# The attention product normalised in PSUM and split group by group, with two key tiles of the product issued together

## What is computed

```python
q, k, v = heads(x @ Wq, 16), heads(x @ Wk, 4), heads(x @ Wv, 4)      # k and v repeated 4 times
attn = softmax(q @ k.T / sqrt(32));  x = layernorm(x + (attn @ v) @ Wo)
w_scale = max(|weight|, axis=1) / 127;   w_q = clip(round(weight / w_scale), -128, 127)
x_scale = max(|x|, axis=2) / 127;        x_q = clip(round(x / x_scale), -128, 127)
x = layernorm(x + (x_q @ w_q.T) * x_scale * w_scale + bias)
```

## Time and profile before

| | us |
|---|---|
| median of 3 runs | 861.05 (860.06 to 861.08) |
| the profiled execution | 858.5 |
| its span, first to last instruction | 856.7 |
| head, before the first exponential of segment 0 | 41.3 |
| segment 0 | 94.2 |
| segments 1 to 6 | 102.8, 98.8, 98.3, 98.5, 98.3, 102.2 |
| segment 7 | 86.3 |
| tail | 36.0 |

### The profile page before, as it was taken

One profiled execution on the slowest core, in us unless ns is written; L12 is line 12 of the kernel. 1 busy time (PEld: TensorE's weight loads), 2 busy tenths in 40 slices (PEclk: granted clock), 3 DMA queues, 4 the chain that ended last, 5 costly groups with the idle time before them and its releaser, 6 DMA issues.

```text
span 856.7 us, 12297 instructions
## 1 busy us (share of the span) xinstructions
PE 774.4 (90%) x3752; PEld 431.5 (50%) x3752; DVE 698.3 (82%) x1131; ACT 494.5 (58%) x904; POOL 607.6 (71%) x673
## 2 busy tenths in 40 slices
PE   7698999899899998999899998999899998899874
PEld 5444554465456644565445654566445653344441
DVE  4689668789987898888988898878988789779667
ACT  3155566565566656666556556656666645556644
POOL 3365487687785878767876797957877877678935
PEclk9889899999999999999999999999999998889995
DMA  7531123042132223232231322322230421300001
GB/s 217 136 116 38 39 60 96 20 112 63 51 112 50 66 72 98 52 79 83 63 100 41 84 63 60 102 60 78 73 102 27 112 63 50 99 26 26 26 25 49
DMA packets 40897, 61.89 MB, mean 72 GB/s; under 512 B 10385, under 2 KB 12433, under 8 KB 40833
## 3 DMA queue, kind: packets, MB, share of 16 engines
q1 hardware_dynamic: 39488, 57.38, 24.3%
q0 software_dynamic: 1344, 3.74, 1.6%
HBM read 20.71 MB, written 8.39 MB: 34 GB/s over the span
## 4 chain that ended last, share of the span: by engine, by line
PE 48%; DVE 18%; issue 15%; POOL 12%; POOLq 3%; ACT 3%; DMA 1%; SPq 0%; DVEq 0%; ACTq 0%
POOL prob_sum L1007 10%; PE front_bank L328 9%; PE s_bank L373 8%; PE st_bank L382 8%; PE o_bank L397 8%; DVE row_max L786 7%; PE tail_bank L328 6%; DVE o_norm L810 3%; PE z_bank L411 2%; POOLq L1016 2%; PE front_bank L335 1%; DVE o_norm L804 1%; ACT probs L612 1%; PE tail_bank L462 1%; DVE one_ish L799 1%
## 5 line engine op out<-in xcount | busy, mean ns | idle before, releaser
L786 DVE TENSOR_REDUCE row_max<-s_bank 128x1 f32<-128x512 f32 x512 | 339.9, 681 | 84.7 <-PE s_bank L373 82.7
L612 ACT ACTIVATE probs<-st_bank 128x512 f32<-128x512 f32 x512 | 293.4, 595 | 190.7 <-PE st_bank L382 183.7
L1007 POOL TENSOR_TENSOR prob_sum<-prob_sum,probs 128x512 f32<-128x512 f32 x248 | 344.2, 1418 | 6.5 <-ACT probs L612 6.3
L382 PE MATMUL st_bank<-q_stack,k_stack 98*128 98x512 f32 x512 | 231.7, 454 | 9.9 <-ACT probs L612 6.2
L373 PE MATMUL s_bank<-k_stack,q_stack 96*128 96x512 f32 x512 | 214.2, 421 | 24.8 <-DVE row_max L786 23.4
L1007 POOL TENSOR_TENSOR prob_sum<-probs 128x512 f32<-128x512 f32 x128 | 170.3, 1356 | 66.7 <-PE z_bank L411 48.0
L382 PEld LDWEIGHTS st_bank<-q_stack,k_stack 98*128 98x128 f32 x512 | 98.5, 193 | 117.2 <-ACT probs L612 77.2
L397 PE MATMUL o_bank<-probs,v_tok 128*32 128x512 f32 x1024 | 143.1, 632 | 0.7 <-ACT probs L612 0.7
L373 PEld LDWEIGHTS s_bank<-k_stack,q_stack 96*128 96x128 f32 x512 | 99.8, 195 | 65.8 <-DVE row_max L786 35.4
L1012 POOL TENSOR_TENSOR rs<-mv,small 128x1 f32<-128x1 f32 x64 | 12.7, 198 | 124.4 <-DVE mv L830 124.4
L328 PE MATMUL tail_bank<-wo_hi,o_hi 128*128 128x512 f32 x112 | 45.9, 410 | 6.5 <-issue 6.5
(11 more groups left out here) (193 smaller groups left out, 1041.2 us busy)
## 6 DMA issues: line engine op xcount, KB each, us to landing
q_stack<-q_parts SPq DMA_DIRECT2D x357, 64.0 KB, 2.0
x_tok<-in_L_attn_x SPq DMA_DIRECT2D x36, 256.0 KB, 3.8
y_sb<-in_L_attn_x SPq DMA_DIRECT2D x28, 256.0 KB, 2.8
out<-u_sb SPq DMA_DIRECT2D x28, 256.0 KB, 2.3
k_stack<-k_parts SPq DMA_DIRECT2D x90, 64.0 KB, 2.0
probs<-in_L_attn_Wq SPq DMA_DIRECT2D x1, 1024.0 KB, 8.3
o_norm<-in_L_attn_Wo POOLq DMA_DIRECT2D x4, 256.0 KB, 7.6
q_stack<-neg_max SPq DMA_DIRECT2D x64, 8.0 KB, 1.8
```

Source lines behind the costliest of these rows:

```text
L382: nc.tensor.matmul(st_bank[:, j % 2, :], k_stack[0:STACK_M, p, j, kt * P:(kt + 1) * P], q_stack[0:STACK_M, i, j, :], start=True, stop=True ...
L612: nc.scalar.activation(probs[:, kt, j, :], st_bank[:, j % 2, :], ACT.Exp, scale=SCALE).then_inc(exp_done, 1)
L786: nc.vector.tensor_reduce(row_max[:, i % 2, j * QT + qt:j * QT + qt + 1], s_bank[:, qt % 2, :], AX_X, ALU.max).then_inc(max_done, 1)
L1007: nc.gpsimd.tensor_tensor(prob_sum[:, j, :], first, probs[:, kt, j, :], ALU.add).then_inc(sum_done, 1)
```

## The change

1. The normalised product never leaves PSUM. `scale_o` reads o_bank directly and writes inv_sum; `correct` and `normalize` write z_bank in place. `o_evacuate`, o_norm and one_ish go.
2. `o_split_hi` and `o_split_lo` read z_bank and work by groups, for the last batch as well, into rings of six slots, o_hi and o_lo. `last_split_hi` and `last_split_lo` go.
3. The maxima are transposed into o_bank instead of z_bank, between two groups.
4. `rescale` and `residual2` write tail_bank in place, and `add_bias` comes last, from the bank to z_sb; u_sb goes, and `normalize2` works in place in z_sb. In the last batch the bias is added by DVE as well, not by POOL.
5. The attention products are issued in twos: those of steps 2n and 2n+1 at unit 8n + 15.
6. The ffn weight comes in four blocks, each prepared at one unit; Wo lies in prob_sum at first. The memsets of freed_mark go.
7. All lists of units are new.

```diff
-PV_AT = 1
+PV_STEPS, PV_LAG = 2, 15
 MIDDLE = dict(
-    sums_pe=(7, 23, 37, 52),
-    inv_act=(7, 24, 38, 53),
-    correct_dve=(9, 25, 40, 54),
-    scale_dve=(9, 26, 43, 55),
-    norm_dve=(11, 33, 44, 59),
-    o_act=(3, 17, 36, 52),
-    max_pe=(10, 27, 42, 55),
-    max_lo_dve=(10, 27, 42, 59),
-    o_hi_act=(11, 16, 34, 45),
-    o_lo_dve=(12, 21, 34, 46),
-    wo_pe=((14, 16), (26, 27, 28), (39, 40), (49, 50)),
-    add_bias_dve=(22, 35, 45, 57),
-    rescale_dve=(24, 36, 47, 60),
-    norm2_act=(29, 44, 52, 63))
+    sums_pe=(7, 23, 39, 53),
+    inv_act=(7, 23, 39, 53),
+    correct_dve=(8, 23, 40, 56),
+    scale_dve=(8, 24, 40, 57),
+    norm_dve=(9, 26, 40, 58),
+    max_pe=(11, 26, 42, 58),
+    max_lo_dve=(11, 27, 43, 60),
+    o_hi_act=(11, 28, 41, 63),
+    o_lo_dve=(11, 29, 42, 63),
+    wo_pe=((9, 13), (26, 27, 28), (40, 41), (49, 51)),
+    add_bias_dve=(24, 38, 47, 61),
+    rescale_dve=(24, 37, 46, 60),
+    norm2_act=(31, 46, 54, 63))
...
             def pv(b, p, s):
                 if kt == 0:
-                    wait(pe, o_read, b * GROUPS + i)
+                    wait(pe, scaled_done, b * GROUPS + i)
+                    pe.wait_ge(ml_done, maxes[0])
...
             def sums(b, i):
-                pe.wait_ge(ml_done, b * GROUPS + i + 2 if not (is_last(b) and i == GROUPS - 1) else B * GROUPS)
+                wait(pe, o_lo_done, b * GROUPS + i)
...
             def max_t(b, i):
-                wait(pe, correct_done, b * GROUPS + i - 1)
+                wait(pe, scaled_done, o_groups[0])
                 pe.wait_ge(max_done, b * UNITS + (i + 1) * QT * NKV)
-                nc.tensor.transpose(z_bank[0:NKV * QT, 0:P], row_max[:, i % 2, :], ident[:]).then_inc(mt_done, 1)
+                nc.tensor.transpose(o_bank[0:NKV * QT, 0:P], row_max[:, i % 2, :], ident[:]).then_inc(mt_done, 1)
...
+            def out_proj_in_turn(b, t, part, parts):
                 if part == 0:
-                    pe.wait_ge(u_done, FREE + b * QT + t)
+                    wait(pe, xb_done, b * QT + t)
+                out_proj(b, t, tail_bank, share(part, parts))
...
-                    if j == PV_AT and s > 0:
-                        pv(b, p, s - 1)
+                    for first in range(0, STEPS, PV_STEPS):
+                        for n in range(first, first + PV_STEPS):
+                            if u == first * NKV + PV_LAG:
+                                pv(b, p, n)
+                            if u + UNITS == first * NKV + PV_LAG and tail:
+                                pv(b - 1, 1 - p, n)
...
-            def o_split_hi(b, p, t):
-                nc.scalar.copy(o_hi[:], o_norm[:, p, :, t * P:(t + 1) * P]).then_inc(o_hi_done, 1)
+            def o_split_hi(b, i):
+                n = b * GROUPS + i
+                act.wait_ge(norm_done, n + 1)
+                if n >= RING:
+                    act.wait_ge(wo_done, ((n - RING) // GROUPS + 1) * QT)
+                nc.scalar.copy(o_hi[:, slot_of(b, i), :], z_bank).then_inc(o_hi_done, 1)
...
-                nc.vector.tensor_tensor(one_ish[:], z_bank, inv_sum[:], ALU.mult).then_inc(correct_done, 1)
+                nc.vector.scalar_tensor_tensor(out=z_bank, in0=z_bank, scalar=-1.0, in1=inv_sum[:], op0=ALU.mult,
+                                               op1=ALU.mult).then_inc(correct_done, 1)
...
-                nc.vector.tensor_tensor(o_norm[:, p, i, :], o_norm[:, p, i, :], inv_sum[:], ALU.mult).then_inc(scaled_done, 1)
+                nc.vector.tensor_tensor(inv_sum[:], o_bank, inv_sum[:], ALU.mult).then_inc(scaled_done, 1)
...
-                nc.vector.scalar_tensor_tensor(out=o_norm[:, p, i, :], in0=one_ish[:], scalar=2.0, in1=o_norm[:, p, i, :],
-                                               op0=ALU.subtract, op1=ALU.mult).then_inc(norm_done, 1)
+                nc.vector.scalar_tensor_tensor(out=z_bank, in0=z_bank, scalar=2.0, in1=inv_sum[:], op0=ALU.add,
+                                               op1=ALU.mult).then_inc(norm_done, 1)
...
+                nc.vector.tensor_tensor(o_lo[:, slot_of(b, i), :], z_bank, o_hi[:, slot_of(b, i), :].bitcast(F32),
                                         ALU.subtract).then_inc(o_lo_done, 1)
...
+                nc.vector.scalar_tensor_tensor(out=w["bank"], in0=w["bank"], scalar=x_scale[:, t, 1:2],
+                                               in1=w_scale[:], op0=ALU.mult, op1=ALU.mult).then_inc(u_done, 1)
...
+                nc.vector.tensor_tensor(w["bank"], w["bank"], w["xn"], ALU.add).then_inc(z2_done, 1)
...
             def add_bias(b, t):
+                dve.wait_ge(z2_done, n + 1)
+                    wait(dve, out_stored, n * 16)
+                nc.vector.tensor_tensor(w["z"], w["bank"], bias[:], ALU.add).then_inc(xb_done, 1)
...
+            def prepare_weight(o):
+                raw = w_turn[o % 2]
+                dve.wait_ge(wf_in[o], 16)
+                nc.vector.tensor_reduce(w_stat[:, 0, o:o + 1], raw, AX_X, ALU.max,
+                                        apply_absolute_value=True).then_inc(w_max_done, 1)
...
+                nc.vector.tensor_scalar(raw, raw, w_stat[:, 2, o:o + 1], ROUND, ALU.mult, ALU.add).then_inc(w_rounded, 1)
+                nc.vector.tensor_scalar(raw, raw, ROUND + QMAX, ROUND + QMIN, ALU.min, ALU.max).then_inc(w_clipped, 1)
```

More of the change, by code:

```diff
@@ L19 @@
 QMIN = -128.0
-FREE = 1
 ROUND = 12582912.0
@@ L790, in max_lo @@
                 dve.wait_ge(mh_done, b * GROUPS + i + 1)
-                nc.vector.scalar_tensor_tensor(out=neg_max[:, 1, :].bitcast(F32R), in0=z_bank[0:NKV * QT, 0:P],
+                nc.vector.scalar_tensor_tensor(out=neg_max[:, 1, :].bitcast(F32R), in0=o_bank[0:NKV * QT, 0:P],
                                                scalar=-1.0, in1=neg_max[:, 0, :], op0=ALU.mult,
@@ L845, in scale_of_x @@
                 nc.vector.reciprocal(x_scale[:, t, 2:3], x_scale[:, t, 1:2]).then_inc(xinv_done, 1)
-            def add_bias(b, t):
-                w, n = buffers(b, t), b * QT + t
-                dve.wait_ge(xn_done, n + 1)
-                if not is_last(b):
-                    dve.wait_ge(out_done, FREE + n)
-                nc.vector.tensor_tensor(w["z"], w["xn"], bias[:], ALU.add).then_inc(xb_done, 1)
             def rescale(b, t):
@@ L928, in segment @@
                             scale_of_x(b - 1, t)
-                        if tail and u == plan["add_bias_dve"][t]:
-                            add_bias(b - 1, t)
                         if tail and u == plan["rescale_dve"][t]:
@@ L934, in segment @@
                             residual2(b - 1, t)
+                        if tail and u == plan["add_bias_dve"][t]:
+                            add_bias(b - 1, t)
                         if tail and u == plan["stats2_dve"][t]:
@@ L1072, in _ @@
                     inv_std(n, t, mv1, mv1_done, rs1, rs1_done)
-                if step == "bias":
-                    w = last_sets[t]
-                    pool.wait_ge(xn_done, n + 1)
-                    nc.gpsimd.tensor_tensor(w["z"], w["xn"], bias[:], ALU.add).then_inc(xb_done, 1)
                 if step == "rstd2":
@@ L1112, in segment @@
                 for u in range(UNITS):
+                    for o in range(KC):
+                        if not tail and u == WEIGHT_LOAD_SP[o]:
+                            load_weight(o)
                     if u == 0:
```

362 lines of the change are left out of this document (169 added, 193 removed).

## The result

| | before | after |
|---|---|---|
| median | 861.07 us (860.06 to 861.47, 4 runs) | 839.12 us (836.5 to 840.5, 4 runs) |
| profiled execution, its span | 858.5, 856.7 | 836.5, 834.7 |
| mean granted clock, as a share of full | 0.958 | 0.973 |

The ratio is 0.9748, with an interval of 0.9722 to 0.9773. The change saves 22 us; the forecast was 44, and 839 lies within the stated range. The sign was right and the size was off by a factor of two, so the question is where the other half of the expected gain went. The profiled execution of after was the fastest of its four, 2.6 us under the median, so what is read from its trace flatters the change by about that much.

A forecast was written before the change was run, and what follows sets the result against it. PE and DVE were both taken as nearly full, each waiting for the other. Six middle segments at 6.2 us (37.2), plus 2.6 first and 3.9 last, gave 43.7 off 858.5: 814.8, as a median 817.4; range 794 to 842.

The forecast's parts named there:

- DVE's 7.3 us: Middle segment: rewritten operations fall from 27.1 to 19.8 us, so DVE goes from 84.3 to 77.0.
- rival (d): DVE writes to PSUM at the upper bound cost 11.5 us a segment; pairs pay little: about 853; chance 0.05.
- POOL's relief: POOL's 48 additions fall to their median, at most some 4 us; nothing in a middle segment, a little in the last.
- The pairs' price: PE, middle segment: paired attention products save 2.6 us and the sums 0.6, together 3.2; a pair takes about 1.88.
- the sum: Middle segments save 3.2 + 3.0 = 6.2 us each, 37.2 in six; 43.7 with first and last segments.
- Of the 5.9 us of DVE-made idle time I take half, 3.0.: Middle segment: of the loader's 5.9 us idle time belonging to DVE, the lighter DVE returns 3.0 us.
- rival (b): Middle segments: all 5.9 us idle and 1.7 us clock loss go, 10.8 each; 790 (795 with half the falls); chance 0.22.
- Rival (a): Behind pairs DVE runs dry, 4 us a segment, eating its lighter load; only the pairs pay: 837; chance 0.22.
- Rival (c): Late handovers on o_bank and z_bank cost 1.8 us each; six of twelve late a segment give 882; chance 0.08.
- the prediction's distances: New waits between placed steps, all costed at nothing; the sums were put 10 or more units behind the low half.
- Head, segment 0, segment 7: Head 0; segment 0 saves 2.6 us by pairs and one sum; segment 7 saves 3.9, of it 1.3 DVE and POOL.
- I call it even: Tail: o_bank copy goes, four bias additions return from POOL to DVE; net zero, with 1 us either way.

The follow-up runs named there:

- run 1: Kernel before with attention products in pairs at its own places: 898.0 us; kernel after with single products again: 862.38 us.
- Run 2: Kernel after with two more matmuls in each of ten projection jobs of a segment: 855.66 us.
- run 3: Kernel after with eight idle DVE reductions added a segment: at the units of the pairs 839.94 us, between them 866.94 us.
- run 6: Fourth transposition of maxima moved: two units later in the kernel before, 862.22 us; one unit earlier in the kernel after, 854.81 us.
- runs 7 and 8: Kernel after: 7, last products re-placed and last batch's bias on POOL, 837.86 us; 8, seven steps moved 847.84, all bias on POOL 833.19, both 834.38.
- run 4: Newton step cut to operations on one column: made from the kernel before 829.22 us, from the kernel after 838.27 us.

## Why the forecast was half right

- **DVE's 7.3 us.** Right: 84.3 to 77.2, every bank form at 0.68 to 0.75 us with almost no spread, POOL's additions near 1.28. Writes to PSUM cost nothing extra, so rival (d) falls. The Trainium skill ("VectorE: DVE Perf Modes", "The TRN2 errata") gives PSUM the larger fixed cost; these rows (0.69 us from bank to bank, 0.680 to 0.681 before) don't show it, as the prediction took it. POOL's relief was undersized, 6.7 us a segment (74.9 to 68.2) for "at most some 4"; it had no price in a middle segment.
- **The pairs' price.** 1.86 us for two, as computed. What of it reaches the end is 2.2 us a segment for pairs at full clock (run 1) instead of 2.6, and 2.2 of PE's busy time with the sums instead of 3.2. Run 2 has PE's time count for somewhat under half at full clock in these segments; the sum had carried PE's prices to the end in full. Why less than half of an added load shows, and most of the pairs' saving, no run tells.
- **"Of the 5.9 us of DVE-made idle time I take half, 3.0."** This is the step that failed. The waits for row maxima are the same length with a DVE 7.2 us lighter, 22.3 and 22.6 us in six segments; the loader's 2.0 before the transposition became 0.9, and 1.8 for xq_sb came. PE's idle time is 36.5 us before and 37.0 after: of 18 us expected none came. The 5.9 were the loader's idle time, which runs a step ahead of the matmuls; PE itself was idle for 98.30 - 92.75 = 5.55 us in that segment, for all causes. Idle time that one engine makes on another is no stock from which a lighter engine pays out: it follows from where the steps stand (run 3: the same 4.4 us cost 0.4 or 4.1).
- **The clock.** I gave rival (b) 0.22 and left its clock out of the forecast. It is nearly half of what the middle gained: 10 of 22.8 us. That part of (b), 1.7 us a segment, was right; its full 5.9 us was wrong. With it in, the full-clock gain of the six segments is 12.5 us against 37.2, so the miss of the sum is larger than the total tells, and that the time lies in the range is in part luck: without those 10 us it would be some 849, above the range's 842.
- **Rival (a)** gives 837 and the kernel took 839, and its "only the pairs pay" is what run 1 shows. But its mechanism isn't what is seen: DVE doesn't stand idle behind the pairs for 4 us more a segment (0.5 before the row maxima), and without the pairs the lighter DVE pays nothing either.
- **Rival (c)** didn't happen at the chosen places (the o_bank wait is 0.5 us), but lies one unit away (run 6), and costs 2.6 us there, not 1.8. One of the prediction's distances was misread: the sums at unit 7 stand 8 units behind the low half at 63, not 10 or more. No wait came of it.
- **Head, segment 0, segment 7.** Segment 0 gave 3.6 for 2.6, but it was clock and not the pairs: at full clock it's 87.6 and 89.4. Segment 7 gave 1.4 for 3.9, within what executions differ; POOL's relief was there (69.7 to 62.6 us) and didn't show.
- **Tail.** "I call it even" was a mis-sized term: +3.3. Nearly all of it is the four products in a row, 3.6 us (with a lag of 15 units the pair of unit 63 meets the one that is due behind the segment, where before one product was left). The bias back on DVE is 0.2 (runs 7 and 8).

What stays open: why 4 to 5 us of DVE are worth 29 us in the old kernel. It may be the load, the waits of DVE for POOL (last section), or that one step left a bad place; run 6 rules out only the place of the fourth transposition. What decides whether a wait of PE makes the clock fall is open too. Before has a wait of 1.6 us at the transposed maxima in each of its six middle segments; a fall comes within 1.5 us after it in the first four, 5 us after it in the sixth, and in the fifth, at this row, none at all:

```profile
618.96 0.27 PE L419 MATMUL z_bank<-ident,row_max 128*16 128x128 f32 x1 [1.59 <-DVE row_max L786]
```

The same waits of 1.1 us in the kernel of run 4 that was made from before have no fall behind them. It is also open what holds a middle segment at about 95 us, which three quite different kernels reach (after, before without the Newton step, after with the bias on POOL) with PE between 89.1 and 91.4 us; the largest wait left there is the loader's for the exponentials, 5.0 us.

## What to carry to other kernels

Multiply a saving by what share of that engine's time reaches the end, and measure that share by adding load, at two different places: here it was somewhat under half for PE's added load at full clock, and a tenth or nine tenths for DVE according to the place. Before counting on a wait, compare it with the idle time of the engine that waits: here that engine's whole idle time was smaller than the sum of the waits. Count lost clock as a term of its own, span times one minus the granted clock, before forecasting; a stall longer by 1.1 us cost 2.6 here. A change of work and a change of places can't be priced apart: in the old lists the same pairs cost 37 us that in the new ones bring 23.

## What the runs showed of the hardware that I had not expected

A DVE operation whose inputs both lie in SBUF can be slow even with almost nothing to do. In the kernel before without the Newton step, line 811 works on one column and 128 values (shortest/median/longest ns), beside line 799 of the same size that reads a bank:

```profile
L811 DVE TENSOR_TENSOR one_ish<-one_ish,inv_sum x32: 150/974/1282, 95.1 to 798.0; 128x1 f32<-128x1 f32 x32
```

```profile
L799 DVE TENSOR_TENSOR one_ish<-z_bank,inv_sum x32: 141/149/159, 81.9 to 797.2; 128x1 f32<-128x1 f32 x32
```

The excess, up to 1.13 us, is the same as line 810's of the kernel before (1.810 less 0.681), whatever the size of the operation. The traces show it to be a wait for the end of POOL's instruction, not a slower stream. One case, DVE's and POOL's rows of the same stretch:

```profile
435.56 0.97 DVE L811 TENSOR_TENSOR one_ish<-one_ish,inv_sum 128x1 f32<-128x1 f32 x1
```

```profile
431.06 5.45 POOL L1007 TENSOR_TENSOR prob_sum<-probs 128x512 f32<-128x512 f32 x4 [2.34 <-PE z_bank L411]
```

POOL's addition ends at 436.51 us, DVE's operation at 436.53. In that kernel 29 of the 32 operations of line 811 start while POOL adds probabilities (or as one addition gives way to the next), and all 29 end 15 to 22 ns after POOL's addition; the other three take 0.150 to 0.165 us. In the kernel before, 28 of the 32 of line 810 start beside such an addition and end 548 to 556 ns after it; the other four take 0.681 to 0.694. Both lines thus end behind POOL in 0.13 us less than they take undisturbed. It works the other way round too: the 92 additions of POOL there that take more than 1.5 us all start while DVE is in an operation with two SBUF inputs. In the kernel after, line 795, with one input in PSUM, runs beside POOL in 28 of 32 cases and takes 0.677 to 0.700 us.

So taking the size out of such an operation, as run 4 did, takes out little of its time; taking away the second SBUF input, as the change does, takes out all of the wait.
